# Two graph-attention layers on one core: edges and rows loaded earlier, the exponent splitting and the search for block tops spread over steps

## The reference

```python
def L0(h, w, a, src, dst):                    # layer 0
    hi, hj = h[src], h[dst]
    e = leaky_relu(concat([hi, hj], -1) @ w, 0.2) @ a
    exp_e = exp(e)
    denom = segment_sum(exp_e, src)
    return segment_sum(hi * (exp_e / denom[src]), dst)

def L1(x, src, tgt, W, A_left, A_right, residual_projection):   # layer 1, 4 heads of 32
    H = heads(x @ W)
    s = leaky_relu((H . A_left)[:, src] + (H . A_right)[:, tgt], 0.2)
    s = exp(s - max(s))
    alpha = s / (segment_sum(s, src)[:, src] + 1e-8)
    agg = segment_sum(alpha * H[:, tgt], src) + x @ residual_projection
    return elu(agg)

x = layernorm(x + L0(x, w0, a0, src, dst))
x = layernorm(x + L1(x, src, dst, ...))
```

## Time and profile before

| | |
|---|---|
| device time, median of 3 runs | 3372.64 us (3370.05 to 3385.1) |
| the profiled execution | 3371.61 us, its span 3369.8 us |
| TensorE busy | 3073.6 us (91%) |
| VectorE busy | 3095.1 us (92%) |
| ScalarE busy | 2725.8 us (81%) |
| GpSimd busy | 159.1 us (5%) |
| mean granted TensorE clock | 0.968 |

### The profile page before, as it was taken

The page is one execution under the profiler, slowest core; times in us unless marked ns, Lnnn a source line. Parts: engine busy times, 40 slices in busy tenths (PEclk is TensorE's granted clock), DMA queues, the critical chain, the costliest instruction groups (busy, mean ns, idle before and its releaser), DMA issues. The chain is left out here.

```text
span 3369.8 us, 100973 instructions
## 1 busy us (share of the span) xinstructions
PE 3073.6 (91%) x39974; PEld 2791.6 (83%) x39974; DVE 3095.1 (92%) x5054; ACT 2725.8 (81%) x6802; POOL 159.1 (5%) x252
## 2 busy tenths in 40 slices
PE   4777689999999999699999999987999999999995
PEld 3666577777777777599999999977999999999994
DVE  7999879998999999899999999978999999999997
ACT  4989777777877777699999999975777777777777
POOL 0000000000000000000000000000111111111110
PEclk9999899999999999799999999998999999999998
DMA  2000022222222222244333333305444445444441
GB/s 63 12 15 12 9 96 90 84 90 85 90 84 85 90 84 72 55 96 96 97 97 97 96 97 97 96 30 182 159 156 156 158 156 158 157 156 158 156 144 40
DMA packets 173164, 333.01 MB, mean 99 GB/s; under 512 B 54849, under 2 KB 108693, under 8 KB 172690
## 3 DMA queue, kind: packets, MB, share of 16 engines
q1 hardware_dynamic: 172690, 326.50, 31.6%
HBM read 320.77 MB, written 5.66 MB: 97 GB/s over the span
## 5 line engine op out<-in xcount | busy, mean ns | idle before, releaser
L942 PE MATMUL l_gathered<-xp,l_src_onehot 128*128 128x128 bf16 x7203 | 466.9, 221 | 11.2 <-DVE l_src_onehot L855 11.2
L647 PE MATMUL sc_z<-sc_onehot,pq 128*128 128x256 f32 (+1 forms) x2450 | 426.5, 296 | 54.5 <-DVE sc_leaky L568 44.9
L1316 PE MATMUL l_gathered<-hp,l_onehot 128*128 128x128 bf16 x7203 | 459.0, 219 | 0.0
L736 ACT ACTIVATE sc_leaky<-sc_z 128x1024 f32<-128x1024 f32 (+3 forms) x325 | 310.1, 954 | 153.0 <-PE sc_z L651 96.3
L942 PEld LDWEIGHTS l_gathered<-xp,l_src_onehot 128*128 128x128 bf16 x7203 | 407.8, 99 | 26.2 <-DVE l_src_onehot L855 11.6
L780 DVE TENSOR_TENSOR l_lane<-iota_b,l_lane_pairs 128x896 bf16<-128x896 bf16 x686 | 421.7, 615 | 0.0
L1330 PE MATMUL l_acc<-e,l_lane_wide 128*128 128x132 f32 x2744 | 399.3, 286 | 16.5 <-ACT e L1385 16.3
L568 DVE SCALAR_TENSOR_TENSOR sc_leaky<-sc_z,sc_leaky 128x1024 f32<-128x1024 f32 (+3 forms) x325 | 369.9, 1138 | 45.6 <-ACT sc_leaky L736 42.2
L1316 PEld LDWEIGHTS l_gathered<-hp,l_onehot 128*128 128x128 bf16 x7203 | 406.7, 98 | 0.4
L651 PE MATMUL sc_z<-sc_onehot,pq 128*128 128x256 f32 (+1 forms) x2450 | 401.0, 286 | 0.0
L647 PEld LDWEIGHTS sc_z<-sc_onehot,pq 128*128 128x128 f32 x2450 | 340.7, 194 | 69.3 <-issue 68.2
(11 more groups left out here) (233 smaller groups left out, 6064.3 us busy)
## 6 DMA issues: line engine op xcount, KB each, us to landing
l_got<-edge_rows_wide SPq DMA_DIRECT2D x343, 448.0 KB, 3.7
l_got<-edge_rows_src SPq DMA_DIRECT2D x343, 224.0 KB, 3.2
placed<-edge_rows SPq DMA_DIRECT2D x144, 512.0 KB, 3.7
out_dram<-X SPq DMA_DIRECT2D x12, 256.0 KB
edge_rows<-bin_bytes SPq DMA_DIRECT2D x98, 6.1 KB
edge_rows_wide<-bin_rows SPq DMA_DIRECT2D x98, 12.2 KB
placed<-edge_rows SPq DMA_DIRECT2D x24, 64.0 KB, 2.8
placed<-edge_rows SPq DMA_DIRECT2D x6, 256.0 KB, 3.6
```

Source lines behind the costliest of these rows:

```text
L647: nc.tensor.matmul(z[:, b, 0:nw, :], PQ[:, b0 + b, q, 0:C], hot[:, r % HOTS, b, 0, 0:nw, :], start=(b == u and q == 0), stop=False)
L736: nc.scalar.activation(y, z, ACT.Relu, scale=1.0 - ALPHA).then_inc(s["positive"], 1)
L942: ins = nc.tensor.matmul(gps[:, t % 2, i * P:(i + 1) * P], hot[:, t % RING, i, :], parts[:, g * GX + i, q, :], start=(q == 0), stop=(q == 2))
L1316: ins = nc.tensor.matmul(gps[:, t % 2, i * P:(i + 1) * P], dst_hot[:, t % RING, i, :], hp[:, g * GX + i, q, 0:C], start=(q == 0), stop=(q ...
```

## The change

- **Opening.** The edges of the first two windows are loaded there already, into spare columns of `e0` (`first_edges`), as soon as the offsets are ready. x is no longer issued by SP behind the weights but by ScalarE's queue, once dst has landed. VectorE and TensorE do the products of the weights ahead of the counting. GpSimd's filling of `SL` is dropped.
- **Binning.** The first chunk is now 2 + 2 + 3 windows. Both first windows are spread on ScalarE at once; the keys of windows 2 and 3 stand behind the first `pick`, those of 4 to 6 behind step 0.
- **Scores.** A function `slots` says at which step after a pair's end each part is done. `split` becomes four operations in four steps: `take_high` and `take_middle` on ScalarE, `take_rest` and `take_low` on VectorE. Kept, turned and exponents two steps earlier, staged four; the items begin at step 11 instead of 13. In the last three pairs two items go into each step, and 9 steps instead of 26 follow the last gather.
- **Projection.** SP loads the first three groups of rows of layer 1 there (`load_rows`).
- **Layer 1.** Absent lanes are excluded by a matmul into the score banks (a diagonal of -1e30 times a row of ones and zeros, `exclude`), the row made by ScalarE (`find_absent`). The search is spread: the first reduction in step g = 3 behind `weigh`, its leaky line in g = 4, the second reduction and line in g = 5, the maximum last in g = 5. GpSimd negates.

```diff
 def bin_windows(...):
-                load(0, slice(0, FIRST), first_read)
-                load(0, slice(FIRST, CHUNK), read[0])
-                load(1, slice(0, CHUNK), read[1])
+                load_windows(sp, k, src, dst, edges[:, 0], 0, slice(FIRST, SECOND), second_read)
+                load_windows(sp, k, src, dst, edges[:, 0], 0, slice(SECOND, CHUNK), read[0])
+                load_windows(sp, k, src, dst, edges[:, 1], CHUNK, slice(0, CHUNK), read[1])
...
-                place_keys(0, slice(0, FIRST), first_read, FIRST)
+                place_keys(0, slice(0, FIRST), k.first_read, FIRST, k.first_edges)
...
-                    if n == -2:
-                        place_keys(0, slice(FIRST, CHUNK), read[0], CHUNK - FIRST)
                     if 0 <= n + 1 < NB:
                         pick(n + 1)
+                    if n == -1:
+                        place_keys(0, slice(FIRST, SECOND), second_read, SECOND - FIRST, edges[:, 0])
...
+                    if n == 0:
+                        place_keys(0, slice(SECOND, CHUNK), read[0], CHUNK - SECOND, edges[:, 0])
 def score_edges(...):
+        def slots(pair):
+            first = (pair + 1) * PER
+            if pair == PAIRS - 2:
+                at = dict(keep=3, turn=4, exponent=5, stage=5, high=6, rest=6, middle=7, low=7)
+                items = [8 + i // 2 for i in range(DEN)]
+            elif pair == PAIRS - 1:
+                at = dict(keep=2, turn=2, exponent=2, stage=1, high=2, rest=2, middle=2, low=2)
+                items = [2 + i // 2 for i in range(DEN)]
+            else:
+                at = dict(keep=3, turn=4, exponent=6, stage=7, high=7, rest=8, middle=9, low=10)
+                items = [11, 12, 12] + list(range(13, 24)) if pair < PAIRS - 3 else [11 + i // 2 for i in range(DEN)]
+            return {n: first + a for n, a in at.items()}, [first + a for a in items]
...
-                    if step == 10 and 1 <= pair <= PAIRS:
-                        split(pair - 1)
+                    for pair in due("rest", r):
+                        take_rest(pair)
+                    for pair in due("low", r):
+                        take_low(pair)
 def norm_and_project(...):
+            @block.sync
+            def _(sp):
+                for u in range(LOADS_1):
+                    load_rows(sp, k, got, wide_rows, u)
 def layer1(...):
+                    nc.gpsimd.tensor_scalar(neg[:, b % 2:b % 2 + 1], k.m_all[:, b:b + 1], -1.0, None, ALU.mult
+                                            ).then_inc(s["negated"], 1)
...
+                def exclude(b, bank, i, j):
+                    nc.tensor.matmul(sps[:, bank, 0:(j - i) * HP].rearrange("p (i c) -> p i c", c=HP)[:, :, 0:HEADS], never[:],
+                                     absent[:, b % 2, i:j].unsqueeze(2).to_broadcast([P, j - i, HEADS]), start=True, stop=False,
+                                     skip_group_check=True)
...
+                def find_absent(b):
+                    if b >= 2:
+                        act.wait_ge(s["scored"], (b - 1) * PER)
+                    nc.scalar.activation(absent[:, b % 2], k.SL[:, 0, 0:NB, b], ACT.Relu, scale=-1.0).then_inc(s["absent"], 1)
 def load_and_place(...):
-                sp.dma_start(X[:, 0:NFULL, :], x[0:NFULL * P].rearrange("(b p) c -> p b c", p=P)).then_inc(k.x_loaded, 16)
-                sp.wait_ge(s["zeroed"], 1)
-                sp.dma_start(X[0:NREST, NFULL, :], x[NFULL * P:N]).then_inc(k.x_loaded, 16)
+                sp.wait_ge(s["offsets"], 1)
+                load_windows(sp, k, src, dst, k.first_edges, 0, slice(0, FIRST_WINDOWS), k.first_read)
+
+            @block.scalar
+            def _(act):
+                act.wait_ge(s["dst_loaded"], 16)
+                act.wait_ge(s["zeroed"], 1)
+                act.dma_start(X[0:NREST, NFULL, :], x[NFULL * P:N]).then_inc(k.x_loaded, 16)
+                act.dma_start(X[:, 0:NFULL, :], x[0:NFULL * P].rearrange("(b p) c -> p b c", p=P)).then_inc(k.x_loaded, 16)
...
-                nc.gpsimd.memset(k.SL[:], -1.0)
```

295 lines of the change are left out of this document (173 added, 122 removed).

## The result

The changed kernel takes 3690.43 us (median of 6 runs, 3683.97 to 3699.43), the kernel before 3373.3 us in the same series (6 runs). The ratio is 1.0943, 95% interval 1.0921 to 1.0966: it is 317 us slower. The forecast was 3327 us, 45 us faster, with a range of 3306 to 3346.

A forecast was written before the change was run, and what follows sets the result against it. TensorE and VectorE were taken as nearly full in layer 1, leaving only mutual waits to gain. 30.6 + 4 + 9.4 + 0 + 1 = 45 us off 3371.6, plus 1 for the median: 3327 us, range 3306 to 3346.

The forecast's parts named there:

- part 1: Layer 1: weighing first, search spread over three steps, exclusion by matmuls, negation on GpSimd; gain 30.6 us, bounds 14 and 36.7.
- Cost 0: Layer 1: GpSimd's negation is done 1.0 to 2.0 us after the top, the exponent comes 2.6 after; 0 us.
- Rival C: Layer 1: exponent waits for GpSimd's negation, each us beyond 2.6 costs 47, over 0.5% slower from 3.9; chance 0.03.
- Part 2: Layer 1's start: three loads of rows move into the stage ahead; gain 4 us, bounds 3 and 6.
- Part 3: Opening: earlier offsets and window loads start keys sooner and remove the second wait; gain 9.4 us, bounds 3 and 12.
- Rival B: Opening: windows queue behind the rows of x, or targets don't land earlier; 6 us lost, 3333 us; chance 0.12.
- Part 4: Score stage: 0 for the middle pairs (bounds -6 and +13), gain 1 us at the end (bounds -3 and 4).
- The term for the clock: Score stage: a shift in time may change how many turns show the lowered clock; 4 us to either side.
- A: Layer 1: VectorE becomes the bound, layer 1 gives 14 to 21 us; 3336 to 3344, at worst 3358; chance 0.17.
- D: Score stage: it follows VectorE after all and gives 0.55 us per pair; 3314 us; chance 0.12.

The follow-up runs named there:

- the third experiment: The changed kernel with GpSimd's lowering of X issued directly behind the reduction, ahead of the negation; 3702.77 us (one run).
- the first experiment: The changed kernel with the negation back on VectorE, a step after the maximum; 3328.24 us against 3373.45 before, ratio 0.9883; repeated at 3335.99 us.

## Why the prediction was wrong

- **The step that failed** stands in part 1: "An operation of GpSimd on 128 columns took 0.97 us beside a busy VectorE; this one has one column, so 0.97 is its upper end", with as much for the reduction. The operation was priced (0.26 measured), the way to it was not. "Cost 0" was -6.15 us of wait and -1.1 of clock per block, some 350 us. The row of 0.97 is the third of three ordinary operations in a row, so it shows no change of kind. The only place in the trace of before where an ordinary operation follows the reduction without another wait between is the first block, and there the price stands in the open:

```profile
2295.91 0.60 POOL L1289 PARTITION_ALL_REDUCE block_top<-l_top  x1 [65.56 <-DVE l_top L1228]
2305.07 0.92 POOL L1292 TENSOR_SCALAR X<-X 128x128 f32<-128x128 f32 x1 [8.55 <-issue]
```

  8.55 us that the profile puts down to nothing. In all other blocks the low sums follow, and their wait for ScalarE (10.97 us) covers it. The instruction that marks the change of kind stood in this trace too, ahead of this very operation (two records, as above):

```profile
L1292 POOLq MODIFY_POOL_CONFIG  x2: 83/83/83, 2296.5 to 2296.5; - x2
```

- **Rival C** had the right wait, the exponent behind the negation, and its formula held nearly: each us beyond 2.6 costs 47. With the 8.7 us measured it gives 47 x (8.7 - 2.6) = 287, plus the clock; only the last 0.6 us in the third experiment cost nothing. Its bound ("2.0 at worst by the row of 0.97") and with it the chance of 0.03 were wrong. The stretching by VectorE that it named is not what happened: the negation took 0.26 us (0.14 on VectorE) and the reduction 0.70 (0.38 in the median before), the wait between them 7.60.
- **The rest of part 1 was right.** Once the negation is back, blocks are 20.11 us apart (20.15 forecast), TensorE has no wait left in them, and the two exclusions cost 0.04 each (steps of 2.90 instead of 2.86), where 0.063 was taken. From the first top to the last it is 31.6 us less than before (963.7 against 995.3), where 30.6 was forecast.
- **Part 2**: layer 1 takes 1001.2 us in the first experiment, 39.9 less than before: 31.6 between the tops, 1.8 behind the last, and 6.5 ahead of the first, where 4 was forecast, just outside the bounds 3 and 6.
- **Part 3**: 7.6 us in the changed kernel (6.1 and 6.9 in the first experiment and its repeat) for 9.4. The offsets came at 16.76 instead of 15.3 (the terms given, 9.7, 4.6 and 0.8, add up to 15.1), because VectorE now waits for the weights (11.39) ahead of counting; the stage followed SP's end by 1.0 us instead of 3.0; the windows landed late beside x (5.7 us from issue), so keys at 25.78, not 23.7. The third find at 35.59 is 8.8 us earlier. Rival B had the right reason, with 2 to 3 us lost instead of 6. The Trainium skill ("DMA: Bandwidth & Descriptors", section "Queues, rings and completion order") says that a DMA engine takes turns between queues packet by packet. The prediction read from it that the windows would land in about the empty time; 5.7 against 1.6 us disagrees with that reading, not with the turns.
- **Part 4**: 0 for the middle pairs holds: behind 22 of the 25 pairs the first experiment is 833.7 us into the stage, the kernel before 833.6. The last two pairs and the tail gain 0.5 us (72.3 to 71.8) for the 1 forecast: the tail behind the last leaky line is 4.3 shorter (13.9 to 9.6), the part ahead 3.8 longer, where 3.3 was taken. The term for the clock, 4 us to either side, took in short dips only; a fall that lasts 82 us, 15.4 lost here, was not among the cases.
- Rivals A and D did not occur: VectorE is busy 98 of 100 us in layer 1 of the first experiment, and TensorE all of it; the pairs of the score stage did not get shorter by 0.55. The ends of the range were 2 us wider than their terms (3314 less 6.1 is 3308, and A ended at 3344).

## What to carry to other kernels

Price the way to an operation, not the operation alone: for an engine that changes between kinds of work, look for the first place in the trace where the new neighbour follows the old one with nothing else to wait for, and read the idle time "<-issue" there. Work on an idle engine is free only while its answer is not awaited, and then all that the engine does in between counts, in both directions. A gap of a few us ahead of TensorE can cost more than its length, since the clock comes back late (5.18 us for a step of 2.86 here).
